# Three exponent tiles of a visit in one ScalarE instruction, in a cross-attention kernel

## What is computed

```python
q = split(hidden @ w_q); k = split(text @ w_k); v = split(text @ w_v)
out_text = merge(softmax(q k^T / sqrt(16)) v)
out_ip   = merge(softmax(q k_ip^T / sqrt(16) + mask_ip) v_ip)
out = (out_text + out_ip) @ w_out + b_out + hidden
```

## Time and profile before

| | us |
|---|---|
| median of 3 runs | 1982.79 |
| lowest and highest run | 1971.43, 1989.99 |
| the profiled execution | 1979.62 |
| its span, first to last instruction | 1977.8 |
| PE busy in it | 1892.0 (96%) |
| DVE busy | 1333.7 (67%) |
| ACT busy | 1203.0 (61%) |

### The profile page before, as it was taken

The page is one execution under the profiler, slowest core; times in us unless marked ns, Lnnn a source line. Parts: engine busy times, 40 slices in busy tenths (PEclk is TensorE's granted clock), DMA queues, the critical chain, the costliest instruction groups (busy, mean ns, idle before and its releaser), DMA issues.

```text
span 1977.8 us, 42926 instructions
## 1 busy us (share of the span) xinstructions
PE 1892.0 (96%) x17944; PEld 760.8 (38%) x17944; DVE 1333.7 (67%) x1665; ACT 1203.0 (61%) x2364; POOL 329.6 (17%) x384
## 2 busy tenths in 40 slices
PE   5897999999999999999999999999999999999897
PEld 2343344333444334443444334433344433444332
DVE  5766776657776677766776676766777667766860
ACT  0165666646666566665666566665666646666674
POOL 4012211111122021121111211112111211111000
PEclk9998999989999899999999999998999989999998
DMA  8515434454554543455443643436445454443401
GB/s 226 85 32 131 79 66 90 77 137 71 81 91 85 131 75 69 87 122 102 71 92 66 145 79 66 79 66 146 78 75 91 83 133 73 78 83 68 86 10 44
DMA packets 95476, 175.62 MB, mean 89 GB/s; under 512 B 38385, under 2 KB 63730, under 8 KB 91442
## 3 DMA queue, kind: packets, MB, share of 16 engines
q1 hardware_dynamic: 86066, 144.55, 38.8%
q0 software_dynamic: 7776, 27.67, 5.6%
q10 hardware_dynamic: 1440, 0.66, 0.1%
HBM read 117.75 MB, written 48.82 MB: 84 GB/s over the span
## 4 chain that ended last, share of the span: by engine, by line
PE 77%; DMA 9%; DVE 6%; SPq 3%; issue 3%; ACT 1%; ACTq 1%; POOLq 0%; POOL 0%; DVEq 0%
PE pv_bank L664 21%; PE max_bank L608 18%; PE work_bank L514 11%; PE work_bank L481 9%; PE exp_bank L648 7%; DMA scratch_q<-q_parts 7%; PE work_bank L492 3%; DVE tile_max L922 2%; PE max_bank L619 2%; PE exp_bank L652 2%; SPq L368 1%; SPq L365 1%; PE work_bank L520 1%; DMA q_stack<-scratch_q 1%; ACTq L814 1%
## 5 line engine op out<-in xcount | busy, mean ns | idle before, releaser
L831 ACT ACTIVATE probs<-exp_bank 128x512 f32<-128x512 f32 x1920 | 1007.2, 598 | 451.0 <-PE exp_bank L648 439.8
L922 DVE TENSOR_REDUCE tile_max<-max_bank 128x2 f32<-128x1024 f32 x632 | 774.4, 1225 | 448.1 <-PE max_bank L608 444.4
L608 PE MATMUL max_bank<-k_stack,q_stack 48*128 48x512 f32 x1896 | 578.8, 474 | 19.1 <-DVE tile_max L922 16.6
L664 PE MATMUL pv_bank<-probs,v_ones 128*17 128x512 f32 x3840 | 532.5, 618 | 0.0
L924 DVE TENSOR_REDUCE tile_max<-max_bank 128x1 f32<-128x512 f32 x632 | 430.5, 681 | 5.8 <-PE max_bank L608 5.7
L648 PE MATMUL exp_bank<-q_stack,k_stack 50*128 50x512 f32 x1920 | 424.5, 406 | 3.1 <-ACT probs L831 3.1
L608 PEld LDWEIGHTS max_bank<-k_stack,q_stack 48*128 48x128 f32 x1896 | 239.0, 187 | 426.6 <-issue 279.9
L481 PE MATMUL work_bank<-ctxt,wk 128*32 128x400 f32 x2560 | 258.1, 510 | 14.5 <-DMA ctxt<-in_ctx_t 11.0
L648 PEld LDWEIGHTS exp_bank<-q_stack,k_stack 50*128 50x128 f32 x1920 | 244.6, 190 | 52.0 <-ACT probs L831 37.7
L514 PE MATMUL work_bank<-wv,ctxt 128*32 128x320 f32 x3072 | 252.3, 439 | 0.8 <-ACT vip L771 0.5
L514 PEld LDWEIGHTS work_bank<-wv,ctxt 128*32 128x32 f32 x3072 | 93.6, 111 | 168.7 <-issue 111.7
(11 more groups left out here) (93 smaller groups left out, 802.2 us busy)
## 6 DMA issues: line engine op xcount, KB each, us to landing
k_stack<-scratch_k SPq DMA_DIRECT2D x240, 200.0 KB, 7.7
scratch_k<-k_parts SPq DMA_DIRECT2D x80, 400.0 KB, 4.7
ctxt<-in_ctx_t POOLq DMA_DIRECT2D x56, 400.0 KB, 11.7
q_stack<-scratch_q SPq DMA_DIRECT2D x240, 64.0 KB, 2.3
scratch_q<-q_parts SPq DMA_DIRECT2D x80, 128.0 KB, 10.6
r_wide<-scratch_r SPq DMA_DIRECT2D x40, 256.0 KB
o_t<-o_sum SPq DMA_DIRECT2D x160, 32.0 KB, 2.0
xres<-in_x SPq DMA_DIRECT2D x8, 640.0 KB, 6.7
```

Source lines behind the costliest of these rows:

```text
L608: nc.tensor.matmul(round_place(n, r)[:, k, :], exact(q_stack[stack, slot, c, t * 128:(t + 1) * 128]), exact(k_stack[stack, slot, c, chunk ...
L664: last = nc.tensor.matmul(pv_bank[h * 32:h * 32 + VW, :], v_ones[:, v_slot(b, kt), head * VW:(head + 1) * VW], p, start=(kt == 0), stop=(k ...
L831: nc.scalar.activation(dst, exp_bank[:, at % BANKS, :], ACT.Exp, scale=SCALE).then_inc(probs_ready, 1)
L922: nc.vector.reduce_max(flat[:, at:at + 2], place[:, 0:2, :], AX.X).then_inc(max_taken, 1)
```

## The change

ACT's function for one exponent tile becomes one for all tiles of a visit. It waits for the last score matmul of the visit, reads `exp_bank[:, 0:count, :]` as one operand of 128 x 1536 (128 x 1024 for the tail), writes 1536 consecutive columns of the ring, and raises `probs_ready` by 3 (or 2) when the whole instruction is done. So that the columns are consecutive, the heads lie in the ring in the order in which they are computed, and the reader looks them up there. The waits on `pv_done` that stood before the first tile of a key tile now stand before the instruction of the visit in which that key tile begins. PE's instructions, their order and their waits in the source stay as they are, as do all transfers.

```diff
-                    p = probs[:, kt % PROB_RING, h, :] if kt < FULL else probs_tail[:, side_of(h)[1], :]
+                    p = probs[:, kt % PROB_RING, HEADS_IN_TURN.index(h), :] if kt < FULL else probs_tail[:, side_of(h)[1], :]
...
-            def exp_tile(group_no, at):
-                act.wait_ge(scores_ready, group_no * EXPS + at + 1)
-                kt, j = at // GH, at % GH
-                if j == 0:
+            def exp_tiles(group_no, v):
+
+                tiles = tiles_at(v)
+                act.wait_ge(scores_ready, group_no * EXPS + tiles[-1] + 1)
+                starts = [at // GH for at in tiles if at % GH == 0]
+                for kt in starts:
...
-                dst = probs[:, kt % PROB_RING, HEADS_IN_TURN[j], :] if kt < FULL else probs_tail[:, j, :]
-                nc.scalar.activation(dst, exp_bank[:, at % BANKS, :], ACT.Exp, scale=SCALE).then_inc(probs_ready, 1)
+                at, count = tiles[0], len(tiles)
+                flat = probs[:, :, :, :].rearrange("p r h n -> p (r h) n")
+                dst = flat[:, at % (PROB_RING * GH):at % (PROB_RING * GH) + count, :] if at < FULL * GH else probs_tail[:, :, :]
+                nc.scalar.activation(dst, exp_bank[:, 0:count, :], ACT.Exp, scale=SCALE).then_inc(probs_ready, count)
...
-                        for at in tiles_at(v):
-                            exp_tile(group_no, at)
+                        exp_tiles(group_no, v)
```

## The result

| | before | after |
|---|---|---|
| median of four runs each, us | 1985.3 | 2018.5 |
| lowest and highest | 1971.4, 1990.0 | 2013.7, 2026.2 |
| span of the profiled execution | 1977.8 | 2020.1 |
| PE busy | 1892.0 (96%) | 1903.5 (94%) |
| ACT busy | 1203.0 (61%) | 1123.9 (56%) |

The ratio is 1.0183, with a 95% interval of 1.0119 to 1.0246. The forecast was 2004, in a range of 1990 to 2032.

A forecast was written before the change was run, and what follows sets the result against it. PE, busy 96%, was taken to set the pace, so ACT's savings gain nothing. Losses of 9.8 + 0.6 + 5.6 + 7.8 = 23.8 us put the kernel at 2003.4 or 2006.6 by base, stated as 2004, range 1990 to 2032.

The forecast's parts named there:

- the instruction: ACT's joined exponential of 1536 columns takes 1.45 us, saving 0.12 us a visit, some 80 us of ACT's busy time.
- its release: In group 20, visit 6, PE's next score load is freed 0.05 us after ACT's end, with 0.02 us left.
- group 37: Losses of visits 3 to 13 hide in visit 14's wait for Q; visits 0 to 2 move transfers: +0.6 us.
- the clock: Rival: longer waits bring 1.2 GHz to groups 38 and 39, 0.74 us more in up to 33 visits; up to 2028; chance 0.08.
- the edge: Rival: 0.1 us more makes some 260 ordinary visits lose 21 us and 58 floor visits 6; about 2031; chance 0.21.
- The sum: All terms over the kernel, 9.8 + 0.6 + 5.6 + 7.8 = 23.8 us slower.
- groups 2, 3 and 4 of seven batches: Short visits 1 and 15 of group 2 and 13 of groups 3 and 4 lose about 1.4 us a batch, 9.8 in all.
- group 38: Its 17 visits go from 35.4 to 41.0 us, eleven short ones rising to 2.28 each: +5.6 us.
- group 39, 16 visits: PE and ACT alternate instead of overlapping, 16 x 2.28 = 36.5 us for 28.7: +7.8 us.
- the subtraction of 0.3 a batch: In other short visits, single waits for a second or third tile go, 0.1 us each; 0.3 taken off per batch.
- The floor: Shortest possible visit, three scores and one ACT instruction without overlap: 0.74 + 0.04 + 1.45 + 0.05 = 2.28 us.
- the 260: Ordinary visits with under 0.03 us left, from about seven a group; they would lose 0.08 each if the edge tipped.

The follow-up runs named there:

- The filler: Against the changed kernel, PE runs four more unread matmuls into max_bank in visits 1 to 15 of group 39; 1.0168 of before.
- 0.31 us later: Against the kernel with late start, late signal and three instructions, ACT takes six instructions of 256 columns; 1.0464 of before.
- late start and signal: Against the changed kernel, three instructions a visit, still waiting for the last score and signalling once at the end; 2025.3 us, 1.0219 of before.
- short visits one by one: Against the changed kernel, tiles of groups 1, 37 to 39 and named short visits are taken and signalled singly; 1986.4 us, 1.0018 of before.
- the late start: Against the changed kernel, ACT still waits for the third score, but takes three tiles and signals each; 1.0118 of before.

## Why the prediction was right, and where it was too small

The mechanism that the forecast rests on was right: the instruction, its release, and where the loss lies. Three things beside it were wrong: what hides the losses of group 37, how much the clock costs, and how near the edge is. The instruction: 1.45 forecast, 1.451 measured. Its release in an ordinary visit: 0.05 us after its end, nothing left, no loss. ACT's saving, 79 us against 80, is worth nothing that can be measured (the two kernels that use it only in ordinary and only in short visits). The loss lies in the visits that were shorter than the cycle of three scores and one instruction, and comes from the lost overlap. Here the rule of the Trainium skill named there ("Perfetto Trace Analysis", section Optimizing Scalar/DVE Operations: break instructions up where an engine that isn't saturated makes others wait) agrees with the runs. That two instructions instead of three are enough is shown by the runs alone.

The sum was 23.8 us. The medians differ by 33.2, and the interval of the ratio is 24 to 49 us, so by time the sum lies at its lower end. The two profiled executions differ by 42.3 in span. The range reached up to 2032 because room was left for the edge and the clock; the sum alone would not have reached the measured time. By the traces:

| term | forecast | measured |
|---|---|---|
| groups 2, 3 and 4 of seven batches | 9.8 | 11.4 |
| group 37 | 0.6 | 3.5 |
| group 38 | 5.6 | 8.8 |
| group 39, 16 visits | 7.8 | 11.4 |
| groups 0 and 1 | 0 | 4.4 |
| all else | 0 | 2.8 |

*Groups 2 to 4* come near the forecast in part by luck, since two errors work against each other. Groups 3 and 4 lost 7.0 us, where 3.8 stood in the list before the subtraction of 0.3 a batch. Group 2 lost 4.5, where 7.9 stood. Visit 1 lost 0.60 us on average and not 0.43, but the visit behind it gave back 0.22, and visit 0 was 0.35 shorter than before, for a reason that stays open.

*The floor* was put at 2.28 and is 2.32: ACT starts 0.09 after the modelled end of the third score (1976.20 + 0.73 to 1977.02), where 0.04 had been taken from the first score. Over some 65 visits that is 2.6 us. For a short visit whose own scores were not held up the floor is higher still, as the maxima between its loads and its third score count too: visit 13 of groups 3 and 4 became 2.43, a loss of 0.42 each instead of 0.27.

*The clock* was a rival with 0.08 and happened in part. Group 39 has five of its 16 visits at 2.82 to 2.99; they are 2.9 us more than the floor, of the 11.4. In group 38 five visits between 3 and 11, at 2.73 to 3.01 and at mean granted clocks of 0.53 to 0.89, are 2.9 us more than the floor; one of them, visit 3, was at 0.74 before as well. Visits 13 to 15 had been put at 7.53 us together and took 8.11: visit 14, put at the floor of 2.28, had lasted 3.01 before and took 3.40, at a granted clock of 0.51. The filler shows the cause for group 39. The price of the rival was too high for each visit: three scores took 1.22 us and not twice 0.74. That rival should not have stood against the forecast but in it: the same waits that make the loss make PE idle.

*Group 37* was to hide its losses in the wait for Q. The transfers did take the same time (11.3 us from store to load before, 11.0 after), but PE stood at L619 for only 1.4 us (from its last score load, 1875.95, to 1877.51), and visits 3 to 13 lost 3.5 us between them. After the change PE comes to L619 0.3 us behind its score loads, without waiting for the transfer. The wait's own length had to be read, not only that it exists.

*The edge* was a rival with 0.21 and priced at 27 us for 0.1 us. It did not tip. Nor were so many visits near it: the 260 came from seven a group, but only groups 3 and 4 of a batch have seven at 2.38 to 2.44, and the whole kernel 188. The kernel with a signal 0.12 us later lost 0.1 us in an ordinary group, a seventh of that price: the start of a weight load is not the last moment at which it may start. At 0.31 us later the price is real.

Groups 0 and 1 took 96.7 to 102.8 us in the eleven profiled kernels without relation to what was changed in them (98.0 with late start and signal, 101.2 with short visits one by one, and 99.9 with the filler, which up to group 39 is the same code as the change with its 102.4), so their 4.4 us are not put down to the change. Group 1 of the first batch has eight visits under 2.30 us, which lose 0.4 to 1.2 each and 5.0 together, but its wait for Q in visit 14 is then 3.7 us shorter. What else varies in these groups stays open.

## What to carry to other kernels

Joining instructions of an engine joins their waits: the joined one starts when its last input is there, and frees the buffer of its first input only at its end. Before joining, find the shortest turn of the loop, not the usual one, and compare it with the cycle of producer and joined consumer without overlap; if the buffer holds just one joined piece, leave one piece separate or give it a second buffer. When a PE that was nearly full is made to wait in a stretch, count its lower clock there as part of the price.

## What the runs showed of the hardware

One Exp over three PSUM banks, 128 x 1536, took 1.451 us, over two 1.023, over one 0.597: 0.83 ns a column, as the copies of 256 and 400 columns inside one bank show, so crossing into a second and third bank cost nothing that shows. Three in a row took 1.57, six of half size 1.76.

A score load of 0.19 us that started 0.12 instead of 0.23 us ahead of its matmul delayed nothing: the matmul came 0.33 us behind those of the maxima, as usual.

PE at the lower clock made three scores in 1.22 instead of 0.73 to 0.76 us. In group 39 the granted clock was 1.00 with PE busy 13.4 of 14.3 us, 0.78 with 30.84 of 40.1, and 0.96 with 32.00 of 38.5. The busy share does not tell the clock by itself: work takes longer at the lower clock, and with the late start PE was busy 36.6 of the 40.0 us from 1934 to 1974 at 0.73.
